# A five-layer attention and expert kernel: key-stage rows normed by ScalarE two batches ahead, the routed attention's tail re-banked, and unread matrix products placed in TensorE's waits

## What is computed

```python
h = _L0_tok_ref(x, ...)
h = h + _L0_attn_ref(_layernorm(h, axis=-1), ...)   # kernel-feature attention, 12 heads, 44 features
h = h + _L0_ffn_ref(_layernorm(h, axis=-1), ...)
h = h + _L1_attn_ref(_layernorm(h, axis=-1), ...)
h = h + _L1_ffn_ref(_layernorm(h, axis=-1), ...)    # attention, then 8 experts, two for each token

# _L0_attn_ref, keys:  stab is one maximum over all keys of all batches
data_dash = jnp.einsum('bhnd,md->bhnm', data_normalizer * data, proj)
diag_data = jnp.sum(jnp.square(data), axis=-1, keepdims=True) * 0.5 * data_normalizer * data_normalizer
return ratio * (jnp.exp(data_dash - diag_data - jnp.max(data_dash)) + EPS)

# _L1_ffn_ref
x = x + _attention(_layer_norm(x, ln1_g, ln1_b), qkv_w, qkv_b, proj_w, proj_b)
xn = _layer_norm(x, ln2_g, ln2_b).reshape(B * N, C)
logits = xn @ gate_w
top_logits, top_idx = jax.lax.top_k(logits, TOP_K)
```

## Time and profile before

| | |
|---|---|
| median of 3 runs | 2306.88 us (2304.25 to 2309.21) |
| the profiled execution, its time | 2306.84 us |
| its span in the trace | 2305.1 us |
| busy over the span: TensorE, VectorE, ScalarE, GpSimd | 1859.0, 1428.0, 1114.0, 458.1 us |
| key stage, products from first to last | 124.05 to 224.00 us |
| routed attention, last block, first value products to the last logits of the loop | 1642 to 1900.6 us |
| its tail | 1900.6 to 1953.2 us |
| routed experts | 1953.2 to 2305.1 us |

### The profile page before, as it was taken

One profiled execution on the slowest core, in us unless ns is written; L12 is line 12 of the kernel. 1 busy time (PEld: TensorE's weight loads), 2 busy tenths in 40 slices (PEclk: granted clock), 3 DMA queues, 4 the chain that ended last, 5 costly groups with the idle time before them and its releaser, 6 DMA issues. The chain is left out here.

```text
span 2305.1 us, 30762 instructions
## 1 busy us (share of the span) xinstructions
PE 1859.0 (81%) x9804; PEld 964.5 (42%) x9804; DVE 1428.0 (62%) x2547; ACT 1114.0 (48%) x1999; POOL 458.1 (20%) x626
## 2 busy tenths in 40 slices
PE   5787989878876417777498978998899983999998
PEld 4643645444334201000122244442133332888887
DVE  6556345452104778999788887999688884222222
ACT  2012335432102758999799964332577760322221
POOL 5000000000211011222100013331034443233333
PEclk9988899978886755555599978996799995999999
DMA  4011211064992006432100009877678723676774
GB/s 88 16 46 43 65 44 35 14 249 178 411 411 99 0 1 198 132 104 95 33 28 27 28 17 157 127 125 105 79 94 114 104 50 125 182 207 195 208 207 106
DMA packets 153844, 262.03 MB, mean 114 GB/s; under 512 B 28640, under 2 KB 124497, under 8 KB 148726
## 3 DMA queue, kind: packets, MB, share of 16 engines
q1 hardware_dynamic: 135366, 242.23, 39.8%
q0 software_dynamic: 18256, 18.19, 4.0%
q10 hardware_dynamic: 96, 0.01, 0.0%
HBM read 217.80 MB, written 58.76 MB: 120 GB/s over the span
## 5 line engine op out<-in xcount | busy, mean ns | idle before, releaser
L1792 PE MATMUL ps<-arena 128*128 x384 | 198.0, 621 | 104.7 <-ACT ps L1834 57.3
L1834 ACT ACTIVATE ps<-ps,arena 128x512 f32<-128x512 f32 x384 | 256.6, 1120 | 6.3 <-POOL arena L1818 6.3
L1802 DVE TENSOR_REDUCE arena<-ps 128x1024 f32 x192 | 232.9, 1225 | 24.0 <-PE ps L1792 9.9
L1834 ACT ACTIVATION_READ_ACCUMULATOR ps<-ps,arena 128x1 f32 x384 | 234.7, 667 | 0.0
L2681 ACT ACTIVATE arena<-ps 128x1024 f32<-128x1024 f32 x192 | 185.2, 1022 | 91.8 <-PE ps L2559 90.7
L2208 DVE TENSOR_REDUCE arena<-ps 128x1024 f32 x192 | 221.0, 1218 | 8.7 <-PE ps L2453 6.3
L3016 ACT ACTIVATE arena<-ps,arena 128x256 f32<-128x256 f32 x234 | 89.5, 481 | 236.7 <-PE ps L2981 236.6
L1999 ACT ACTIVATE arena<-ps 128x1024 f32<-128x1024 f32 x192 | 178.7, 1046 | 8.0 <-DVE arena L2019 4.6
L2453 PE MATMUL ps<-arena 96*128 96x512 bf16 x500 | 163.8, 433 | 21.2 <-DVE arena L2208 11.7
L3047 DVE SCALAR_TENSOR_TENSOR arena<-ps,arena 128x192 f32<-128x192 f32 x78 | 29.0, 413 | 233.4 <-issue 233.4
L2951 POOL DMA_INDIRECT out_dram<-arena x78 | 121.3, 1555 | 238.7 <-DVE arena L3047 155.0
(11 more groups left out here) (406 smaller groups left out, 3298.6 us busy)
## 6 DMA issues: line engine op xcount, KB each, us to landing
arena<-in_sm_w_dram SPq DMA_DIRECT2D x128, 576.0 KB, 15.3
arena<-in_re_w_dram SPq DMA_DIRECT2D x39, 1252.0 KB, 5.8
arena<-ra_parts SPq DMA_DIRECT2D x192, 192.0 KB, 9.3
routed_in<-routed_in SPq DMA_DIRECT2D x8, 3332.0 KB, 14.2
ra_parts<-arena SPq DMA_DIRECT2D x48, 192.0 KB, 2.4
arena<-la_xt SPq DMA_DIRECT2D x16, 512.0 KB, 3.6
arena<-routed_in SPq DMA_DIRECT2D x39, 196.0 KB, 5.5
arena<-arena SPq DMA_DIRECT2D x64, 96.0 KB, 2.2
```

The source lines that it names most:

```text
L1792: ins = pe.matmul(ps[:, 2 * (n % 4) + t % 2, :], QM[j][:, h, t * P:(t + 1) * P], KI[:, b, h // HG, :], start=True, stop=True)
L1802: v.tensor_reduce(MXq[:, b, 2 * u:2 * u + 2, at_head(h)], ps[:, 2 * (n % 4):2 * (n % 4) + 2, :], AX.X, ALU.max).then_inc(s_lk, 1)
L1834: ins = act.activation(bank, bank, ACT.Exp, bias=nb[n % 4][:, t % 2:t % 2 + 1], scale=c_reg, accum_out=RS[:, b, t, at_head(h):at_head(h) + 1])
```

## The change

Three places are edited. (1) In the key stage ScalarE norms the rows, with `(x * rstd) + shift`, where VectorE once computes `shift = -mean * rstd` for all batches. There are two buffers `XN`, so the rows of batch b + 2 are normed in batch b, in two halves between ScalarE's squares; TensorE turns batch b + 1 behind tile 0, and ScalarE copies it before square 1. (2) In routed attention ScalarE copies the logits: in the loop before its exponential 2 of the next batch, and `add_stream` keeps only VectorE's add. For the last batch TensorE projects head groups 0 and 1 as soon as they are normalised, into four banks, and group 2 when it is there; the ranks of batch 6 follow both halves. (3) 34 matrix products of 128 by 512 that nothing reads (`keep_busy`) stand before the waits of the tail, and two more before the first transposition of the experts. ScalarE loads the table of Gelu at the end of routed attention.

```diff
-    XN = g1(P, [T, D + R])
+    XN = [g1(P, [T, D + R]) for _ in range(2)]
+    shift = g1(P, [B, T])
...
+            def norm(b, tiles):
+                if b > 1 and tiles[0] == 0:
+                    xt.wait(act, b, -1)
+                for t in tiles:
+                    for at, of in ((0, slice(0, D)), (D, slice(P, D))):
+                        w = of.stop - of.start
+                        ins = act.activation(XN[b % 2][:, t, at:at + w], m.H[:, b, t, of], ACT.Identity,
+                                             bias=shift[:, b, t:t + 1], scale=m.rstd[:, b, t:t + 1])
+                if tiles[-1] == T - 1:
+                    ins.then_inc(xn.sem, 1)
+
+            act.wait_ge(s_sh, 1)
+            norm(0, range(T))
+            norm(1, range(T))
             copy(0)
             for b in range(B):
                 square(b, 0)
-                square(b, 1)
                 if b + 1 < B:
                     copy(b + 1)
+                square(b, 1)
+                if b + 2 < B:
+                    norm(b + 2, (0, 1))
                 square(b, 2)
+                if b + 2 < B:
+                    norm(b + 2, (2, 3))
                 square(b, 3)
...
-                    if t == 0 and b + 1 < B:
-                        norm(b + 1)
...
-            norm(0)
+            v.scalar_tensor_tensor(out=shift, in0=m.mean, scalar=-1.0, in1=m.rstd, op0=ALU.mult, op1=ALU.mult
+                                   ).then_inc(s_sh, 1)
...
-                    if t == 1 and b + 1 < B:
+                    if t == 0 and b + 1 < B:
                         turn(b + 1)
...
-                lc.wait(sp, p, 1)
+                sp.wait_ge(s_add, p + 1)
...
+            def keep_busy(n):
+                for _ in range(n):
+                    pe.matmul(ps[:, 5, :], m.ident, m.H[:, 0, :, :].rearrange("p t d -> p (t d)")[:, 0:512], start=True,
+                              stop=True)
+
             ex.wait(pe, B - 1, 2 * NS)
-            project(B - 1, 7, 0)
-            ranks(B - 2, 5)
-            project(B - 1, 3, 1)
+            sh.wait(pe, B - 1, 1)
+            for g in range(NG):
+                if g == NG - 1:
+                    keep_busy(3)
+                    ot.wait(pe, B - 1, 1)
+                for t in range(T):
+                    ins = pe.matmul(ps[:, t, 0:D], OT[:, g, t * P:(t + 1) * P], Wp[:, g, :], start=(g == 0),
+                                    stop=(g == NG - 1))
+                    if g == NG - 1 and t % 2:
+                        ins.then_inc(pr.sem, 1)
+            ranks(B - 2, 4)
+            keep_busy(8)
             xa.wait(pe, B - 1, 1)
-            turn_rows(B - 1, 0, 0)
-            turn_rows(B - 1, 1, 2)
+            lc.wait(pe, B - 2, 1)
+            turn_rows(B - 1, 0, 6)
+            turn_rows(B - 1, 1, 7)
+            keep_busy(1)
             logits(B - 1, 4)
+            keep_busy(2)
             po.wait(pe, B - 2, 1)
-            ranks(B - 1, 5)
+            ranks(B - 1, 4)
+            keep_busy(20)
...
+            def logits_copy(p, bank):
+                lp.wait(act, p, 1)
+                if p:
+                    mk.wait(act, p - 1, 1)
+                act.activation(LG, ps[:, bank, 0:T * NX].rearrange("p (t n) -> p t n", t=T), ACT.Copy).then_inc(lc.sem, 1)
+
             for b in range(B):
                 for e in range(2 * NS):
+                    if b > 1 and e == 2:
+                        logits_copy(b - 2, 6 + b % 2)
...
+            act.preload_act_table(ACT.Gelu)
...
-            def logits(p, bank):
-                v.tensor_tensor(m.H[:, p, :, :], m.H[:, p, :, :], X[p % 2], ALU.add)
+            def add_stream(p):
+                v.tensor_tensor(m.H[:, p, :, :], m.H[:, p, :, :], X[p % 2], ALU.add).then_inc(s_add, 1)
                 if p == B - 1:
                     scale_last()
-                lp.wait(v, p, 1)
-                v.tensor_scalar(LG, ps[:, bank, 0:T * NX].rearrange("p (t n) -> p t n", t=T), 1.0, None, ALU.mult
-                                ).then_inc(lc.sem, 1)
...
+            for _ in range(2):
+                pe.matmul(ps[:, 7, :], m.ident, m.H[:, 0, :, :].rearrange("p t d -> p (t d)")[:, 0:512], start=True,
+                          stop=True)
             turn_rows(0)
             turn_rows(1)
```

More of the change, by code:

```diff
@@ L535, in _ @@
             xc.start(act)
+            xn.start(act)
             act.wait_ge(s_bd, 1)
@@ L563, in _ @@
         def _(v):
-            xn.start(v)
             kd.start(v)
-            def norm(b):
-                xt.wait(v, b, 0)
-                for t in range(T):
-                    for at, of in ((0, slice(0, D)), (D, slice(P, D))):
-                        w = of.stop - of.start
-                        ins = v.tensor_scalar(XN[:, t, at:at + w], m.H[:, b, t, of], m.mean[:, b, t:t + 1],
-                                              m.rstd[:, b, t:t + 1], ALU.subtract, ALU.mult)
-                ins.then_inc(xn.sem, 1)
             def batch(b):
@@ L2790, in _ @@
                     if b and g == 2:
-                        logits(b - 1, 7 - j)
+                        add_stream(b - 1)
                     av.wait(v, b, T * (g + 1))
```

28 lines of the change are left out of this document (18 added, 10 removed).

## The result

The changed kernel takes 2284.73 us (median of 6 executions, 2281.19 to 2297.53), the kernel before beside it 2307.09 (6 executions, 2304.25 to 2309.23): ratio 0.9902, interval 0.9884 to 0.9920, or 22.4 us less. 2282.8 was forecast. The profiled execution took 2287.18 us, its span is 2285.4. The forecast is 1.9 us off, but the trace shows that two larger errors cancel in it: what was edited gained more than forecast, and stages that nobody touched gave part of it back.

The account below looks back on a forecast made before the run. The prediction saw a chain of stages bound by waits between engines and a falling TensorE clock. Gains of 18.5 (key stage), 2.3 (loop) and 3.2 us (tail) sum to 24.0, from 2306.84 to 2282.8 us; range 2276 to 2292.5.

Parts of the forecast that it names:

- The period: Key stage: with TensorE's 2.01 us wait gone, a batch with a transposition takes 9.79 us.
- 1.3 us later: Key stage start: ScalarE's first norm and making `shift` delay the start by 1.3 us, bounds 0.2 and 2.3.
- Rival (b): Key stage: the clock keeps falling three or four times, 1.6 us a fall, giving 2288.4 us; chance 0.09.
- of the six batches that have ranks three are of each kind: 3 x 0.77 = 2.3 us: Routed loop: three batches without a clock fall each gain TensorE's 0.77 us wait; three with a fall gain nothing.
- if the clock stays up ... 2.2 us earlier: Tail: at full clock VectorE reads batch 6's ranks 2.2 us earlier; if the clock falls, the gain is 0.3 us.
- the step on GpSimd's four sends: Tail: GpSimd's inverse deviation stands behind four sends awaiting batch 6's places, so the layer norm gains 2.2 or 0.3 us.
- they keep the clock up: Tail: eight unread products hold the clock, so one transposition takes 0.61 us and the logits 1.95; gain 2.0 us.
- rival (d): Tail: unread products run at 1.2 GHz, the tail ends 25 us later, total 2311 us; chance 0.03.
- an unread product is still running when a wait ends: Tail and experts' start: a stated sign that the prediction is wrong; no size given.
- Nothing was taken for the two products: Experts' start: two uncovered products cost 2.1 to 3.7 us, offset by faster tiles; net zero, at most 2.5 us loss.
- if a stage that nobody touched changes its length with the clock: Unedited stages: a stated sign that the prediction is wrong; no size given.
- 3.2 us of work: Tail: a clock that falls at 1901.8 returns after some 3.2 us of work; the gain is then 0.3 us.

Follow-up runs that it names:

- kernel 1: The kernel before with the edit of the key stage alone, everything behind it as before: 2293.61 us, ratio 0.9936.
- kernel 5: The kernel before with two row buffers and the norm kept on VectorE but made two batches ahead: 2287.37 us, ratio 0.9909.
- kernel 10: The kernel before with the routed loop's edit alone (ScalarE copies the logits, stream stored behind its addition): 2304.66 us, ratio 0.9982.
- 3: The changed kernel without any of its unread products, in the tail and before the experts: 2290.02 us, ratio 0.9914.
- 7: The changed kernel with GpSimd's inverse deviation two sends earlier and one unread product instead of three ahead of the last group: 2280.15 us, ratio 0.9866.
- kernel 2: The changed kernel with the key stage of before; loop, tail and experts stay changed: 2297.86 us, ratio 0.9956.
- 11: The changed kernel with VectorE norming two batches ahead, GpSimd's inverse deviation two sends earlier, one unread product ahead of the last group: 2273.21 us, ratio 0.9839.
- kernel 8: The changed kernel with two more unread products (the bridge) ahead of the soft expert stage's first dispatch transposition: 2282.04 us, ratio 0.9886.
- 9: The changed kernel again with no change, for a second profile and more executions: 2283.34 us, ratio 0.9880.

## Why the prediction held, step by step

**Key stage: mechanism right, bounds too narrow.** 18.5 us was forecast with bounds of 17.5 to 19.6; it is 19.0 in the profile, and the stage ends from 19.0 to 22.3 us sooner in the six further profiles with ScalarE's norm two batches ahead, beyond 19.6 in five of them. The period was right to 0.1 us. The scatter comes from where the clock rises in the stage's start, for which the bounds had no term (the prediction let the clock rise "as before"): the products begin at 124.92 us here, at 123.76 in kernel 1, at half speed in both, and the transposition behind tile 0 then takes 1.97 us here and 1.09 there. "1.3 us later" for ScalarE's first norm is 1.27 by kernel 5. Rival (b), a clock that keeps falling, did not come: it is at 1.00 from 140 to 200 us, with 1.1 us of transpositions in each batch. The Trainium skill (TensorE: Matmul & The Clock Gate, section "Part 4: PE-mode transpose") says that these do not count as busy in the same way as products; by it falls were possible, and this trace shows none.

**Loop: mechanism right, size wrong.** The step "of the six batches that have ranks three are of each kind: 3 x 0.77 = 2.3 us" took the number of falls for a property of the kernel. A batch without a fall gained what was said (33.4 to 32.6), a batch with one gained nothing (34.2 both times; 33.9 in the loop's last period), but the falls went from 1 to 3 in the four kernels without the edit to none in seven of the ten with it, and 2, 2 and 4 in the others. The term measured 4.3 us in the first profile, 0.9 in the second, 7.5 in kernel 10. That removing the wait of 0.77 us made falls rarer is what these counts suggest; no run isolates it.

**Tail: too small where the clock held.** 3.2 us was forecast, within 2.3 to 4.2; 6.0 up to the barrier (5.8 to the last ranks) was found in the first profile, 2.1 to the last ranks in the second. The step "if the clock stays up ... 2.2 us earlier" came out at 3.5: VectorE's reading of batch 6's ranks stood 10.2 us behind the loop's last copy, and now some 6.7, 0.9 of it only because the loop's last logits were late by a fall (see 3). From there to the transpositions nothing changed, 9.4 and 9.3 us, as the step on GpSimd's four sends said. From the transpositions on 2.3 us were gained where I said 2.0. But "they keep the clock up" is not reliable: of the eight profiles with the eight unread products, three kept full clock up to the last ranks, four lost it in the products ahead of the ranks, one ahead of the logits. Then the products cost what rival (d) feared, though only a microsecond and not twenty. The prediction's own sign of being wrong, "an unread product is still running when a wait ends", thus came, and also in the first profile: VectorE ends the last normalisation at 1891.2, and TensorE's passes begin at 1892.48, behind the three unread products. By 7 that one cost nothing, since the chain there is GpSimd's.

**Experts: right.** Nothing was taken for the two products, and 0.1 us is what they cost at the stage's start.

**What failed: untouched stages at nothing.** The prediction named it as a way to be wrong, "if a stage that nobody touched changes its length with the clock", and gave it no chance and no price. It cost 10.5 us in the profile. Touched parts gained 30.2 us where I said 24.0. Without the cancellation the forecast would have missed by six in this execution, at 2276.6 and so below its own range: that it came within 2 us is luck. The medians say the same: the key stage alone gained 15.4 us where 18.5 was forecast, loop, tail and experts 11.2 where 5.5 was. They sum to 26.5, and the whole gained 22.4 and 26.9 in two sets of executions.

What ties the give-back to the shift: without the bridge, the six profiled executions whose soft stage began between 466.0 and 475.1 us took 61 there, the six that began up to 464.9 or from 483.7 took 54.2 to 56.4. In all six the clock had risen to 1.00 just ahead of the stage's first idle gap and fell within a microsecond of TensorE's going on; in four of the other six (the kernel before, 2, 5 and 11) it was still at 0.50 in the gap and rose some 6 us behind it. But the remaining two, 1 and 10, also show the rise, the gap and the fall, and there the clock was back after some 3 and 7 us instead of 13 to 17, with stages of 54.9 and 54.4. So a gap behind the rise comes with the fall and does not settle how long it lasts; kernel 8 is the one test of a bridge. What sets the instants and the length of the fall stays open. The prediction took a fall to last 3.2 us of work, from the earlier trace rows; this one is longer. The 3.5 us of the next stage are open too: its length (186.9 to 192.0) follows neither, and kernel 2 shows 2.9 of them without the shift.

## What to carry to other kernels

When an engine is late once a period and not slow, buy it lookahead (a second buffer, the work issued a period earlier) before moving its work elsewhere: here that alone gave the whole gain of the key stage, and moving cost a microsecond at the start. Unread products in a wait must be sized for half clock: where the wait is shorter than they are at that speed, they are in front of the work that they should help. And a stage that follows a shift of some 20 us can change its length by 7 us with the clock, nothing in it being edited, so read gains from the stage's borders, and give the untouched stages a term of their own in the range.

## What had not been expected of the hardware

TensorE worked 14 us without any idle time at a granted clock of 0.50 (window 470 to 484), just behind a stretch at full clock and a gap of 2.3 us, and the second profile of the same kernel (9) shows the same window at 0.50; in the earlier trace rows a fall was over within microseconds. A product of 512 columns takes 0.46 us a pass at full clock (2.74 us for six) and 0.84 mostly at half (3.36 for four at the experts' start). The changed kernel's ten executions spread from 2275.5 to 2297.5 us, all those of the kernel before from 2301.7 to 2315.2.
